# Four attention layers on one core: VectorE adds the maxima in layer 3 of both batches, the last P.V sum runs in pieces of 512, 256 and 256 tokens, and the step order is new

## What is computed

```python
xn = group_norm(x, 32 groups) * gn_w + gn_b
q, k, v = split(qkv_w @ xn + qkv_b)
sim  = q.T @ k * c ** -0.5             # 1024 x 1024, contraction over 128 channels
attn = softmax(sim, axis=-1)
out  = out_w @ (attn @ v) + out_b + x  # the kernel's output
```

## Time and profile before

| | |
|---|---|
| median of 3 runs | 362.13 us |
| the profiled execution, own time | 361.89 us |
| its span on the core | 360.1 us |
| outside the span | 1.8 us |
| busy PE / DVE / ACT / POOL | 332.9 / 244.2 / 192.3 / 70.9 us |
| instructions PE / DVE / ACT / POOL | 1752 / 325 / 236 / 45 |

### The profile page before, as it was taken

One profiled execution on the slowest core, in us unless ns is written; L12 is line 12 of the kernel. 1 busy time (PEld: TensorE's weight loads), 2 busy tenths in 40 slices (PEclk: granted clock), 3 DMA queues, 4 the chain that ended last, 5 costly groups with the idle time before them and its releaser, 6 DMA issues.

```text
span 360.1 us, 4578 instructions
## 1 busy us (share of the span) xinstructions
PE 332.9 (92%) x1752; PEld 148.8 (41%) x1752; DVE 244.2 (68%) x325; ACT 192.3 (53%) x236; POOL 70.9 (20%) x45
## 2 busy tenths in 40 slices
PE   8888878989999996889999999989999999999994
PEld 5443232323424442334443444554443334555442
DVE  2799888777688757598876544985993054498514
ACT  3544479776866268735647528047136912704430
POOL 5000000000005750000000165404010002610970
PEclk9875799999999999999999999999999999999998
DMA  7100000000000000000000000000000000001001
GB/s 289 44 0 2 0 1 2 1 2 0 2 0 0 2 0 0 3 1 4 0 4 0 2 0 0 2 0 1 2 3 2 2 0 2 0 0 59 3 0 58
DMA packets 1437, 4.44 MB, mean 12 GB/s; under 512 B 168, under 2 KB 520, under 8 KB 1288
## 3 DMA queue, kind: packets, MB, share of 16 engines
q1 hardware_dynamic: 1416, 4.15, 3.1%
HBM read 2.99 MB, written 1.05 MB: 11 GB/s over the span
## 4 chain that ended last, share of the span: by engine, by line
PE 71%; DVE 16%; ACT 8%; issue 4%; ACTq 0%; DVEq 0%
PE attn_acc L1011 15%; PE attn_acc L1005 10%; PE products L968 7%; PE products L972 6%; DVE neg_max L699 6%; ACT probs L567 5%; PE products L957 4%; PE products L918 4%; PE products L884 3%; PE products L888 3%; DVE neg_max L696 3%; PE products L896 2%; PE products L1060 2%; DVE neg_max L702 2%; PE products L931 2%
## 5 line engine op out<-in xcount | busy, mean ns | idle before, releaser
L567 ACT ACTIVATE probs<-products 128x1024 f32<-128x1024 f32 x120 | 118.1, 1026 | 59.6 <-PE products L980 25.6
L699 DVE TENSOR_REDUCE neg_max<-products 128x2 f32<-128x1024 f32 x64 | 75.7, 1220 | 17.1 <-PE products L918 17.0
L421 POOL TENSOR_TENSOR prob_sum<-prob_sum,probs 128x1024 f32<-128x1024 f32 x24 | 56.6, 2358 | 64.5 <-ACT probs L567 62.3
L1011 PE MATMUL attn_acc<-probs,v 128*128 128x512 f32 x128 | 63.5, 609 | 0.0
L421 POOL TENSOR_TENSOR prob_sum<-probs 128x1024 f32<-128x1024 f32 x4 | 9.5, 2366 | 213.5 <-ACT probs L567 197.8
L1005 PE MATMUL attn_acc<-probs,v 128*32 128x512 f32 x384 | 50.7, 614 | 0.0
L702 DVE TENSOR_REDUCE neg_max<-products 128x1 f32<-128x1024 f32 x32 | 37.6, 1220 | 8.9 <-PE products L923 6.7
L696 DVE TENSOR_REDUCE neg_max<-products 128x4 f32<-128x1024 f32 x32 | 37.3, 1218 | 3.4 <-PE products L931 3.2
L1011 PEld LDWEIGHTS attn_acc<-probs,v 128*128 128x128 f32 x128 | 22.5, 189 | 21.3 <-issue 18.3
L972 PE MATMUL products<-rows_a,rows_b 128*128 128x512 f32 x64 | 29.7, 600 | 0.5 <-DVE neg_max L696 0.5
L723 DVE RECIPROCAL recips<-products 128x128 f32<-128x128 f32 x10 | 9.6, 957 | 24.9 <-PE products L1031 24.8
(11 more groups left out here) (144 smaller groups left out, 396.7 us busy)
## 6 DMA issues: line engine op xcount, KB each, us to landing
w<-w_rest SPq DMA_DIRECT2D x1, 1236.5 KB, 8.0
x<-x SPq DMA_DIRECT2D x2, 512.0 KB, 4.8
tmp<-row_selector SPq DMA_DIRECT2D x1, 512.0 KB, 8.8
y<-x SPq DMA_DIRECT2D x1, 512.0 KB, 2.6
y<-x SPq DMA_DIRECT2D x2, 256.0 KB, 2.0
w<-w_first SPq DMA_DIRECT2D x1, 147.0 KB, 2.2
rounded_a<-max_rows SPq DMA_DIRECT2D x8, 4.0 KB
max_half_rows<-max_rows SPq DMA_DIRECT2D x4, 4.0 KB
```

Source lines behind the costliest of these rows:

```text
L421: engine.tensor_tensor(DS[:, :], first_in, P[:, n % NP, :], ALU.add).then_inc(den_acc, 1)
L567: nc.scalar.activation(P[:, n % NP, :], slot(s), ACT.Exp, scale=SCALE[L]).then_inc(read_act, 1)
L699: nc.vector.tensor_reduce(out=m[:, 2 * t:2 * t + 2], in_=slot(s).rearrange("p (a n) -> p a n", a=2), op=ALU.max, axis=AX.X, negate=True).t ...
L1011: mm = nc.tensor.matmul(acc[:, h], V13[b][:, t0, :], P[:, b_no[q] % NP, h], start=t0 == first, stop=t0 == last)
```

## The change

Three edits.

1. `SHIFTED` now holds layer 3 of both batches. For batch 0 there is one `spread` step, then 8 B steps without the L980 matmuls, with a DVE add each, and an exponential from SBUF.
2. `PIECES` splits the last attention's token axis in 512, 256 and 256. PV1 runs over the 8 tiles once for each piece. The third piece is written to `acc[:, 0:256]`, the bank of the first piece, after `oh` has evicted that. The last `out` step is gone. ACT copies the second half of the spread reciprocals to `MB`, and for pieces 2 and 3 DVE multiplies `acc` in PSUM with `MB` and then adds to x, 256 columns each. There are three output DMAs.
3. `ORDER` is new (472 steps instead of 464).

```diff
-SHIFTED = ((3, 1),)
+PIECES = (slice(0, 512), slice(512, 768), slice(768, 1024))
+SHIFTED = ((3, 0), (3, 1))
...
-                ("PV1", L, b, g, t, 1) for t in range(8)]
+                ("PV1", L, b, g, t, i) for i in (1, 2) for t in range(8)]
...
-        steps["P"] += [("out", L, b, g)]
+        if (L, b) != LAST:
+            steps["P"] += [("out", L, b, g)]
...
                 elif kind == "bcast" and (L, b) == LAST:
-                    for i, h in enumerate(halves):
+                    for i, h in enumerate(PIECES):
                         sp.wait_ge(x_upd, x_no[(3, b)] + i)
                         sp.dma_start(out[b][:, h], X[b][:, h]).then_inc(out_done, 16)
...
-                elif kind == "out" and (L, b) == LAST:
-                    u = s[1:]
-                    act.wait_ge(pv_done, pv_done_at[("B", *u, 7)])
-                    nc.scalar.activation(O[o_tile[u]][:, halves[1]], acc[:, halves[1]], ACT.Identity).then_inc(acc_out, 1)
+                elif kind == "bcast" and (L, b) == LAST:
+                    wait_tile(act, s)
+                    wait_read(act, ("B", L, b, s[3], 7))
+                    nc.scalar.activation(MB[:, halves[1]], slot(s)[:, halves[1]], ACT.Identity).then_inc(recips_out, 1)
...
-                        for i, h in enumerate(halves):
+                        for i, h in enumerate(PIECES):
                             if i == 0:
                                 dve.wait_ge(half_out, 1)
+                                link(nc.vector.tensor_tensor(T[:, h], o[:, h], slot(s)[:, h], ALU.mult))
                             else:
-                                dve.wait_ge(acc_out, out_no[("out", L, b, g)] + 1)
-                            link(nc.vector.tensor_tensor(T[:, h], o[:, h], slot(s)[:, h], ALU.mult))
+                                dve.wait_ge(pv_done, piece_pv[i])
+                                dve.wait_ge(recips_out, 1)
+                                sums = acc[:, h] if i == 1 else acc[:, 0:h.stop - h.start]
+                                link(nc.vector.tensor_tensor(T[:, h], sums, MB[:, h], ALU.mult))
...
-                        q, h = ("B", L, b, g, t0), halves[s[5]]
+                        q, h = ("B", L, b, g, t0), (PIECES if (L, b) == LAST else halves)[s[5]]
                         wait_probs(pe, q)
-                        mm = nc.tensor.matmul(acc[:, h], V13[b][:, t0, :], P[:, b_no[q] % NP, h],
+                        if s[5] == 2 and t0 == 0:
+                            pe.wait_ge(half_out, 1)
+                        to = acc[:, 0:h.stop - h.start] if s[5] == 2 else acc[:, h]
+                        mm = nc.tensor.matmul(to, V13[b][:, t0, :], P[:, b_no[q] % NP, h],
                                               start=t0 == first, stop=t0 == last)
```

More of the change, by code:

```diff
@@ L94 @@
 ORDER = (
-    "NNVAAANAANAVAAAATAAABABABABAAAPBAPTBBAABAPBBAABAPA"
-    "BABAPPTVBAAPBABBABPBABABPTPABPBBAPABAPBABPPABBPABP"
-    "TBBAPAAPAPBBAAEEBPTBEBBPBBNNVBAPABAABAPABPAPBABPTA"
-    "BAPBABBAPAAPBPPAABPPAABPPPBAAPPPTBBAPPABPABAPBBPTE"
-    "PPBBEBBNBPBBNBPPBNNPPVBPABAPBAPAAPPAAEAETNEBBABAPA"
-    "ANNBBABAAPABAPTBAVABBBAPPABBAPABBABETPPPPEBEBPBEYB"
-    "EPNPPNBBPPPPNNBBPAAAPAPAPAPAPPEPAEPTVNBNBBNNPNPAPA"
-    "APAABAAPVAPATAPAAAPPBBABABABPTPBBBBBBBBPPPBBBEPPPP"
-    "EPEYEBENPPNBBNNBAAAPAPAPAPAPAPEPTVETBBBBBPBPPBBPPP"
-    "PPPPPPPEPPPEPP"
+    "NNVAAANANVAAAAAATAAABABABABAABAPTBAAPBABAPBABABPTP"
+    "ABAPBAPBABABABAPBABABTPBAPAPBABAPBBBAPBABPBAPPTBAB"
+    "PABAPBAPPVABEBEBBBEPBAPANNTVABABABAPABABAPPABPATBP"
+    "BABPBAPPBBAPPBAAPPBAAPPABAPPTBAAPBAPPBBAPPABAPPEBP"
+    "PTBEBBNBPBBNPPBBPNNBBPPABAPBAPAVAPPAAEAETNEBBABAPA"
+    "ABBABAPAANNBBATPAAVABBBAPPABBBAPABBETPPPPEBEBPBEYB"
+    "EPPPNNBPPPPNNBBPAAPAAPAPBAPAPAPEPPTEVTNBNBBPPNNNBA"
+    "PVAPAAAAPAPAAPPATAAPABBABBAPABPTBBBPBPBBBBPBBBPEPP"
+    "PEPEYEBENPNBBNNBAAPAPAPAAPPAAPPETVTBBBBPBPBBEBPPPP"
+    "PPPPPPEPPEPPPPPPPPPPPP"
 )
@@ L218, in attention_layers @@
             free.append((o_tile[u], u))
-    pv_done_at = {}
+    pv_done_at, piece_pv = {}, []
     n = 0
     for s in plan:
-        if s[0] == "PV1" and s[1:3] == LAST and s[4:] == (7, 0):
+        if s[0] == "PV1" and s[1:3] == LAST and s[4] == 7:
             n += 1
-            half_pv = n
-        if s[0] == "PV4" or s[0] == "PV1" and s[5] == 1:
+            piece_pv.append(n)
+        elif s[0] == "PV4" or s[0] == "PV1" and s[5] == (2 if s[1:3] == LAST else 1):
             n += 1
@@ L318, in attention_layers @@
         half_out = sem("half_out")
+        recips_out = sem("recips_out")
         recip_done = sem("recip_done")
@@ L359, in acc_free @@
         def acc_free(L, b, g):
-            i = plan.index(("out", L, b, g))
+            i = plan.index(("oh" if (L, b) == LAST else "out", L, b, g))
             uses = [p for p in plan[:i] if p[0] == "out" and (L or p[1] or p[3] % 2 == g % 2)]
@@ L574, in _ @@
                     u = s[1:]
-                    act.wait_ge(pv_done, half_pv)
+                    act.wait_ge(pv_done, piece_pv[0])
                     last = o_last.get(o_before.get(u))
@@ L1008, in _ @@
                     else:
-                        q, h = ("B", L, b, g, t0), halves[s[5]]
+                        q, h = ("B", L, b, g, t0), (PIECES if (L, b) == LAST else halves)[s[5]]
                         wait_probs(pe, q)
-                        mm = nc.tensor.matmul(acc[:, h], V13[b][:, t0, :], P[:, b_no[q] % NP, h],
+                        if s[5] == 2 and t0 == 0:
+                            pe.wait_ge(half_out, 1)
+                        to = acc[:, 0:h.stop - h.start] if s[5] == 2 else acc[:, h]
+                        mm = nc.tensor.matmul(to, V13[b][:, t0, :], P[:, b_no[q] % NP, h],
                                               start=t0 == first, stop=t0 == last)
-                    if kind == "PV4" or s[5] == 1 or (L, b) == LAST and t0 == 7:
+                    if kind == "PV4" or s[5] == (2 if (L, b) == LAST else 1) or (L, b) == LAST and t0 == 7:
                         mm.then_inc(pv_done, 1)
```

2 lines of the change are left out of this document (1 added, 1 removed).

## The result

| | before | after |
|---|---|---|
| median | 361.96 us (4 runs) | 366.19 us (4 runs, 364.07 to 367.02) |
| ratio | | 1.0105, 95% interval 1.0077 to 1.0134 |
| span of the profiled execution | 360.1 us | 362.3 us (364.07 us, the fastest of the four) |

The change makes the kernel 1% slower, 4.2 us by the medians, 3.8 by the ratio. One of the four runs before, 367.68 us, was a slow one and is not in the ratio; the others took 361.64 to 362.13 us. Forecast were 364.4 us and "within 2%"; the range, 359.2 to 367.8, holds the result.

What follows compares the result with a forecast made beforehand. It took DVE as the bound during the maxima of layer 2, batch 1 and at the start of layer 3, batch 1, and PE from B.3100 on. 361.89 + 0 + 0.4 + 0 + 2.1 = 364.4 us; range 359.2 to 367.8.

Steps and rivals of the forecast that it cites:

- term 1: First four shifted tiles, before and among layer 2, batch 1's maxima: +0.4 us, bounds -1.2 and +2.
- Term 0: New order of steps in layers 0 to 2: taken as 0, with 2 us either way.
- Term 2: Second four shifted tiles, up to the maxima at A.3100: 0 us, bounds -0.9 and +1.2.
- Term 3: The end, from the start of B.3100: +2.1 us net, low end -0.6, high end +3.8.
- out.301: At the end, PV1.31000 must wait for out.301, now behind B.3103's add on DVE: a new 0.9 us wait.
- Lock: At the end, bcast.301's add to x and GpSimd's sums block each other: 1.2 us PE wait, bounds 0 and 2.4.
- bcast.310: At the end, bcast.310 waits for the reciprocals, now less covered by PV1 steps: 0.6 us more.
- The forecast's low end: Lowest outcome for the end: only bcast.301 costs and B.3100 starts 0.6 us early, giving -0.6 us.
- S: Start of B.3100, from which the end is counted: earlier by 0.3 us, bounds 0 and 0.6.
- PE's relief passing through: Rival: PE's 3.1 us saving and 1.2 us at the end are won, less 0.3: 357.9 us; chance 0.17.
- The maxima carry the whole delay: Rival: no gap closes among layer 2's maxima, first four shifted tiles cost +1.7 to +2: 365.9 us; chance 0.12.
- The order of layers 0 to 2 weighs most, by other waits or another stretch at 1.2 GHz: Rival: reordering layers 0 to 2 shifts time 2 us or more either way, 361 or 367.5 us; chance 0.08.

Runs made afterwards that it cites:

- the shift alone: Kernel before in its old order, with only batch 0 of layer 3 also shifted: 362.63 us (10 runs), ratio 1.0030.
- the idle matmuls: Kernel before with 14 idle matmuls of 256 columns, computing nothing, before A steps of layer 0: 362.62 us (10 runs), ratio 1.0020.
- the product in PSUM: Changed kernel with bcast.301's product left in its PSUM slot, so the add to x has one PSUM input: 366.49 us (4 runs), ratio 1.0098.
- the kernel with the old head: Changed kernel with the first 336 ORDER entries (layers 0 to 2) as in the kernel before: 365.54 us (6 runs), ratio 1.0094.

## Why the prediction was right, and where it was not

- **What bounds the kernel, and unit costs: right.** B.3014 also stands in front of y.21, so term 1's stretch has five shifted tiles. By the forecast's unit costs that is 5 x 0.46 less 0.6 for the spread, 1.7 us; measured were 2.0 with the new order and 1.8 with the shift alone. 16 adds of 1.22 us; an instruction of 256 columns costs half of one of 512 (5.45 us for 24, less the drain, 0.22 each), as assumed.
- **Term 0, taken as 0, was the mis-sized step.** Alone it is +2.1 us, just beyond the 2 us that I allowed. The prediction argued that "moving PE steps about wins or loses little" from a stretch where DVE is full. That is right for that stretch, as the idle matmuls showed, but the cost lies behind it: 0.6 us between y.20 and bcast.110, and drops of the clock in places where the profiled execution of before had none. In the changed kernel's own profiled execution the term came out at -1.25, by its early start; that this execution, 364.07 us, lies at the forecast of 364.4 is luck. The median lies in the range because the range was wide enough for what term 0 and term 1 left out.
- **Term 1: +0.4 forecast, +0.45 without and +1.65 with the drop of the clock.** The forecast delay of the first maximum, 2.65 us, was 2.1, and it doesn't come from the adds alone: with the shift alone it is 1.3 us, with the new order and no shift also 1.3. All gaps among the first thirteen closed. But of the steps behind only the run of DVE was counted, and not that PE, now waiting for it in several places at once, would run at 1.2 GHz when the row ended. That is the second failed step, 1.2 us.
- **Term 2: 0 forecast, +0.2.** Right.
- **Term 3: +2.1 forecast, +1.6.** The last PV1 ends 3.0 us later (3.3 forecast). out.301: 0.73 us of wait, 0.9 with the drain (0.9 forecast). Lock, with the wait before den.310: 0.58, and 0.34 in the last PV1 of piece 0, which waits for B.3107's exponential (the x18 row takes 7.37 us, with the product in PSUM 7.03); forecast were 1.2 and 0.3. bcast.310: 0.70 (0.6). The start of B.3100 came 0.45 us earlier (0.3), and spread.31 in front of it waited 0.26 us for the DMA of the maxima. The end behind the last PV1 is 1.4 us shorter (1.2). The forecast's low end, -0.6, does not follow from its own entries: bcast.301 at +0.6, S at -0.6 and -1.2 behind the last PV1 give -1.2.
- The lock: the add ran from 342.85, 16.5 us behind the start of B.3100 (16.6 forecast), and took 3.02 us. The Trainium skill ("SBUF — State Buffer", section "Who interferes with whom") says that the second of the two stands still while the first runs; the traces agree, with 3.02 us for 1.28 and 15.65 for 14.84, and with 1.28 us for the form that reads PSUM. Both sides are seen: the sum that was running when the add started ended at 344.78, and the next one, issued at 344.93 while the add ran on to 345.87, took 3.16 us instead of 2.36.
- **The rivals.** PE's relief passing through (357.9) did not happen: idle time of PE took it all. "The maxima carry the whole delay" named 365.9 us, near the result, and has the size right (+1.65 for +1.7) but the wrong cause: among the first thirteen the gaps did close. "The order of layers 0 to 2 weighs most, by other waits or another stretch at 1.2 GHz", at 0.08, deserved far more.
- **The sum.** 361.9 + 2.1 (order alone) + 1.65 + 0.2 + 1.6 = 367.5 us, above the median of 366.19 and near the slowest execution, 367.02. So the parts overlap somewhat, as the kernel with the old head showed too (it won 0.65, not 2.1). How they overlap is open: four to six executions that differ by up to 3 us don't resolve it.

## What to carry to other kernels

An instruction moved in a long hand-made order is not free because the work is the same: time each reordered stretch alone, and cut both traces at common instructions before costing the edits in them. Where an engine is relieved of work in front of another that is full, count the idle time that arises as well as the busy time that goes; here, with the shift alone, 1.8 us of matmuls gone came with 2.8 us more of waiting. Put waits of TensorE where nothing needs it at full speed behind them, and keep an add from SBUF to SBUF out of a chain of GpSimd's that the end waits for, or give it one input in PSUM.
